# Mask rows loaded in pairs between the stores of the projected parts, and two scatters a step in the last attention group

## What is computed

```
x = ln(x + mamba(x))          # selective scan, 256 inner channels, 16 states
x = ln(x + moe_dense(x))      # 8 experts, the best 2 by softmax, plus a shared one
x = ln(x + attention(x))      # 16 heads of 8, causal
x = ln(x + moe_sparse(x))     # 64 experts, the best 4 of each token, 128 slots an expert
```

## Time and profile before

| | |
|---|---|
| runs | 1644.73, 1650.65, 1650.91 us; median 1650.65 us |
| profiled execution | 1646.96 us, its span 1645.1 us |
| granted TensorE clock, mean | 0.892 of full speed |
| busy: PE, DVE, ACT, POOL | 1332.7, 1200.2, 916.3, 943.3 us |
| scatters of line 1995 | 128, 127.3 us busy on POOL |
| affine selects of line 2011 | 128, 82.7 us busy on POOL |

### The profile page before, as it was taken

The page is one execution under the profiler, slowest core; times in us unless marked ns, Lnnn a source line. Parts: engine busy times, 40 slices in busy tenths (PEclk is TensorE's granted clock), DMA queues, the critical chain, the costliest instruction groups (busy, mean ns, idle before and its releaser), DMA issues. The chain is left out here.

```text
span 1645.1 us, 25186 instructions
## 1 busy us (share of the span) xinstructions
PE 1332.7 (81%) x7232; PEld 716.4 (44%) x7235; DVE 1200.2 (73%) x2215; ACT 916.3 (56%) x1728; POOL 943.3 (57%) x779
## 2 busy tenths in 40 slices
PE   6848888888888989999926999999999998812756
PEld 2313333333333358898913244443343343212743
DVE  6999999999999554224477988889889886260325
ACT  5746666665666554456555076675666566601423
POOL 2478899988998117360756021214563654874773
PEclk9879899999999988999957599999999999955867
DMA  2019100000000025787728211211321114301317
GB/s 70 0 59 345 56 0 0 0 0 0 0 0 0 1 61 141 205 240 199 208 55 256 60 32 37 56 31 31 83 55 35 50 35 106 60 10 47 106 51 257
DMA packets 123041, 124.87 MB, mean 76 GB/s; under 512 B 31182, under 2 KB 97979, under 8 KB 120304
## 3 DMA queue, kind: packets, MB, share of 16 engines
q1 hardware_dynamic: 101032, 99.70, 21.8%
q0 software_dynamic: 10240, 15.79, 3.3%
q10 hardware_dynamic: 11656, 8.00, 1.6%
HBM read 78.52 MB, written 50.91 MB: 79 GB/s over the span
## 5 line engine op out<-in xcount | busy, mean ns | idle before, releaser
L2106 DVE TENSOR_REDUCE t_negm<-t_ps 128x1 f32<-128x512 f32 (+4 forms) x624 | 370.0, 642 | 56.7 <-PE t_ps L2374 35.2
L2083 ACT ACTIVATE t_PT<-t_ps_s 128x1024 f32<-128x1024 f32 (+3 forms) x384 | 292.1, 811 | 203.6 <-PE t_ps_s L2393 202.6
L493 POOL TENSOR_TENSOR s_HC<-s_H,X 128x1024 f32<-128x1024 f32 x128 | 307.0, 2416 | 40.3 <-DVE s_H L614 30.1
L658 PE MATMUL ps_y<-s_HC,ident 128*128 128x512 f32 x512 | 270.5, 655 | 19.8 <-POOL s_HC L493 17.9
L2011 POOL TENSOR_SCALAR_AFFINE_SELECT t_PT<-t_PT 128x512 f32<-128x512 f32 x128 | 82.7, 646 | 276.7 <-ACT t_PT L2083 276.2
L2374 PE MATMUL t_ps<-heads 96*128 96x512 bf16 (+3 forms) x640 | 201.3, 341 | 9.4 <-DVE t_negm L2106 7.6
L2393 PE MATMUL t_ps_s<-heads 96*128 96x512 bf16 (+3 forms) x768 | 181.0, 329 | 3.7 <-ACT t_PT L2083 2.1
L2408 PE MATMUL t_ps_c<-t_PT,t_VG 128*32 128x512 f32 (+3 forms) x1536 | 164.7, 502 | 1.7 <-ACT t_CT L2039 1.1
L554 ACT ACTIVATE s_dA<-m_DT,s_A 128x512 f32 (+1 forms) x192 | 127.4, 711 | 60.3 <-DVE s_H L614 59.4
L658 PEld LDWEIGHTS ps_y<-s_HC,ident 128*128 128x128 f32 x512 | 98.4, 204 | 124.1 <-issue 69.9
L1995 POOL DMA_INDIRECT slots<-X,t_idx_s x128 | 127.3, 994 | 34.9 <-issue 34.2
(11 more groups left out here) (347 smaller groups left out, 2367.2 us busy)
## 6 DMA issues: line engine op xcount, KB each, us to landing
f_w<-in_W_dram SPq DMA_DIRECT2D x93, 256.0 KB, 5.2
heads<-token_expert_rows SPq DMA_DIRECT2D x8, 1024.0 KB, 9.6
token_expert_rows<-X SPq DMA_DIRECT2D x42, 192.0 KB, 2.6
heads<-q_parts SPq DMA_DIRECT2D x42, 192.0 KB
heads<-k_parts SPq DMA_DIRECT2D x14, 576.0 KB
expert_rows<-X SPq DMA_DIRECT2D x27, 192.0 KB, 2.5
f_XS<-expert_rows SPq DMA_DIRECT2D x19, 256.0 KB
expert_rows_out<-f_YB ACTq DMA_DIRECT2D x19, 256.0 KB, 3.6
```

What stands on the lines that cost most here:

```text
L493: nc.gpsimd.tensor_tensor(HC[:, g % RING], H[:, g % RING], row_wide(C_sb[:, g % RING, :], 2), ALU.mult).then_inc(s_hc, 2)
L658: nc.tensor.matmul(ps_y[c][:], ident[:], HC[:, g % RING, c, :], start=g == 0, stop=g == N - 1, skip_group_check=True).then_inc(s_y, 1)
L2083: nc.scalar.activation(PT[:, n % RP, 2 * p:2 * p + 2, 0:wd], src, ACT.Exp, scale=DK ** -0.5).then_inc(s_exp, 1)
L2106: nc.vector.tensor_reduce(out, ps_1[use % BANKS1][:, 0:h * width].rearrange("p (h k) -> p h k", h=h), AX.X, ALU.max, negate=True).then_inc ...
```

## The change

It changes the place of six mask loads and of twelve scatters. The loads of group 0 stay where all eight stood; those of groups 1, 2 and 3 go behind the stores of batches 0, 1 and 2. In group 15 a step may send two scatters.

```
         def _(sp):
             sp.wait_ge(keep["s_md"], 32)
-            for g in range(NG):
+
+            def mask(g):
                 for x, own_rows in enumerate((Q[g], K[g])):
                     sp.dma_start(own_rows[MASK_AT:P].rearrange("r j t -> r (j t)"), keep["mask_rows"][x]).then_inc(keep["s_mr"], 16)
+            mask(0)
             sp.wait_ge(s_z, 1)
...
                         rows = dram["k"][b, a] if x else dram["q"][b, :, a]
                         sp.dma_start(rows.rearrange("d h t -> h d t"), homes[b][:, x, a, :]).then_inc(s_d[b], 16)
+                if b + 1 < NG:
+                    mask(b + 1)
...
-                    if gi * NB + n >= (NG * (sent // (QTR * TOPK) + 1) + SCATTER[0]) * NB + SCATTER[1]:
-                        scatter(sent)
-                        sent += 1
+                    for _ in range(2 if gi + 1 == TG else 1):
+                        if gi * NB + n >= (NG * (sent // (QTR * TOPK) + 1) + SCATTER[0]) * NB + SCATTER[1]:
+                            scatter(sent)
+                            sent += 1
```

## The result

| | before | after |
|---|---|---|
| runs (us) | 1644.73, 1646.75, 1650.65, 1650.91 | 1668.44, 1670.41, 1672.47, 1673.06 |
| median | 1648.70 | 1671.44 |
| profiled execution, its span | 1646.96, 1645.1 | 1672.47, 1670.6 |
| granted TensorE clock, mean | 0.892 | 0.889 |
| GpSimd busy | 943.3 | 942.5 |

GpSimd's total says nothing of it: the same 128 scatters and 128 masks are done in the same busy time. What changed is their order, and only timelines show that.

A forecast was written before the change was run, and what follows sets the result against it. GpSimd's in-order queue was taken to bound the last group and tail, the DMA queues the projection block. 1646.96 + 14.4 + 4.0 = 1665.4, or 1669.1 from the median 1650.65; forecast between them 1667, range 1657.8 to 1671.7 us.

The forecast's parts named there:

- late last pair: Attention start: TensorE waits for all eight mask loads; the last pair lands 2.5 us after the third batch's stores.
- last mask later: Last group: eleven added scatters ahead of the last mask in GpSimd's queue make it end about 13.2 us later.
- slack: Tail: the fourth batch's first scatter could start at 1458.28 but GpSimd gets there at 1459.59; 1.3 us to win.
- clock: Start of the tail: TensorE falls to 1.2 GHz, its rows grow by at most 3.3 us; 2.5 taken.
- no room: Projection block: DMA queue full, so stores and last mask pair land later and TensorE starts the attention 5.8 us later.
- all room: Projection block: DMA queue has all the room needed, only the gain of 1.1 us in ScalarE's wait is left.
- idle share: Projection block: DMA share 0.84 leaves 0.16 of 21 us, 3.4 us; 1.8 us taken as usable.
- first batch's stores land sooner: Projection block: these stores no longer queue behind masks, so ScalarE's wait shrinks by 1.1 us at most.
- from their issue to the block's end: Projection block: four mask loads ahead of the third batch's stores make these land 5.0 us later.
- Queues with room: Projection block: first part neutral or a gain of up to 1.1 us, time 1660.3 to 1661.9; chance 0.24.
- A group that covers the scatters: Last group: masks run while scatters are worked off, the group keeps its length; 1644.6 to 1650.7 us; chance 0.08.
- Half cover: Last group and tail: scatters overlap somewhat more or the tail catches up; +5 to +10 us, 1652 to 1660; chance 0.06.

The follow-up runs named there:

- masks alone: Kernel before with only the mask loads moved in pairs between the stores, one scatter a step: 1654.85 us, ratio 1.0020.
- wait by group: Kernel before with the mask loads moved as in the change, TensorE waiting for each group's own loads by separate semaphores: 1653.68 us, ratio 1.0023.
- the clock held longer: Kernel before with two scatters a step in the last group, plus unused matmuls in its last four steps and around the context transposes: 1663.67 us, ratio 1.0085.
- the scatters placed: Kernel before with the last group's twelve scatters sent one a step, then two in steps without masks, then none: 1650.20 us, ratio 0.9991.

## Why the prediction was right

The forecast was 1667 us, slower, with ends of 1657.8 and 1671.7; the time is 1671.44, by the median 22.7 us more, where the terms summed to 18.4. In the trace the parts are 15.62 and 5.82 us, where 14.4 and 4.0 were taken. GpSimd's queue and the late last pair worked as forecast; several terms had a wrong size, and one path of the first part was missing. That the time lies inside the ends is in part luck: both parts came out above the upper ends given to them (15.2 and 5.8 us), and the upper end of the whole starts from a median of 1650.65 us, 2 us above the 1648.70 of the four runs.

**Second part, by its steps.** The last mask: 13.2 us later was forecast, 34.77 - 21.56 = 13.21 came. That is GpSimd's queue in program order, shown by taking the masks out of it. The tail then adds up from rows:

| term | forecast | measured |
|---|---|---|
| last mask later | 13.2 | 13.21 |
| GpSimd's slack ahead of the fourth batch's first scatter | -1.3 | -0.77 |
| clock | 2.5 | 2.86 |
| first scatter to the end of the block (46.58, now 46.91) | 0 | 0.33 |
| sum | 14.4 | 15.63 |

The **slack** was taken as 1459.59 - 1458.28, with 0.30 us from the weights to the scatter, the distance of two scatters in a row. A GpSimd that waits takes 0.84, so the chain could not have released it before 1457.98 + 0.84 = 1458.82: 0.77 us. The step that failed used the spacing of a busy queue for a restart after a wait. For the **clock** the sum of the rows was a little high (at most 3.3 us: 0.4, 0.4, 0.5 and 2.0 were forecast, 0.23, 0.46, 0.46 and 1.71 came), and the step "part of it lies beside ScalarE's copies" failed: nothing of these lay beside, since every row from the last product on waits for the one before it. From the last mask's end to the projection's start it is 1461.57 - 1456.50 = 5.07 us against 3.92 before, and the projection itself took 1.71 us more: 1.15 + 1.71 = 2.86. The 0.33 was not forecast: in after four scatters of the first half hold GpSimd for 1.17 to 1.22 us, where before two took 1.20 and one 1.04, all while VectorE was at work.

**First part, by its steps.** The forecast took "no room" as +5.8 and "all room" as -1.1, and took off half the idle share (half of 3.4 is 1.7, not 1.8): +4.0. The whole change showed +5.82 and the masks alone +5.12, both nearer to "no room". But the terms behind +5.8 are not those that came, and their errors cancel:

| term | forecast, no room | whole change | masks alone | wait by group |
|---|---|---|---|---|
| first batch's stores land sooner | -1.1 | none | none | none |
| third batch's stores issued later, behind ScalarE | 0 | 1.71 | 1.54 | 1.58 |
| from their issue to the block's end | 5.0 | 2.77 | 2.11 | 1.01 |
| last pair (forecast: 5.8 less the 3.9 of the block's end) | 1.9 | 1.34 | 1.47 | not waited for |
| sum | 5.8 | 5.82 | 5.12 | 2.59 |

Two steps failed. The 1.1 us that ScalarE's wait could lose were never there, since 3.7 us is the stores' plain landing time (six masks fewer ahead of them left a wait of 0.88 us). And the price of four loads, 5.0 us of queue ahead of the stores, was too high as such, while the path over ScalarE was not in the forecast: its issue of the head loads takes longer with mask loads in between and holds back chunk 4. Whether taking 1.8 us off for the idle share was wrong is not settled: the block's end moved by 2.6 to 4.5 us in three traces of the same loads. A share of 0.84, averaged over 16 engines and 4 us, did not say which.

The Trainium skill (DMA: Bandwidth & Descriptors, "Why a DMA increments its semaphore by 16 and not by 1") led to +5.8 by the rule that a transfer uses as many of 16 engines as divide its outer sizes. The total agrees with +5.82, but over other terms, so it is no test of the rule; that the head loads filled 12 of 16 engines is shown by no run here.

**The rivals.** Queues with room, 1660 to 1662: struck out by a start 5.82 us later, released by the mask rows. A group that covers the scatters: struck out by the masks that start where the second scatter ends. The Trainium skill (same page, "Anatomy of one DMA — SWDGE (gpsimd) path") would have had many descriptors go out before a cost shows; the trace disagrees with 0.97 us held for each scatter from the first pair on. Half cover: struck out by 13.21. Of the signs of being right, all came but two. TensorE's start at 909.61 lies past "901 to 906", though 3.95 us of it had passed before the first mask load; without them it is 905.66. And GpSimd's wait is 16.85 us where "about 13" was said: it has the clock term of 2.86 in it, and the restart.

**What stays open.** Why the masks alone cost 3.3 us in the times and 5.1 in the trace (the interval holds both), why the stores' landing differs by 2 us between the traces of the masks moved with one wait and with four, and why ScalarE's issue of the head loads takes longer with mask loads between the stores.

## What to carry to other kernels

An instruction that fills an idle gap on an in-order queue delays everything queued behind it: look for what other engines wait for behind it (here eight masks) before the gap, and place the filler where none follows (the steps without a mask) or take the awaited work off that engine. Before moving work forward, read the most it can win: here the fourth batch's first scatter could start at most 0.77 us earlier, against a price of 13 us. And loads that everybody waits for belong ahead of other transfers in their queue as long as they hold up nothing there (eight in front cost nothing that these traces show). Moving them between stores can also slow the issue of another engine that sends transfers, here ScalarE; a mean DMA share below 1 does not show that there is room.

## What the runs showed of the hardware

- A GpSimd scatter that waited for VectorE started 0.84, 0.85 and 0.84 us after the producing instruction ended (after, the clock held longer, the scatters placed), while scatters in a row stand 0.30 us apart.
- Some scatters held GpSimd for up to 1.22 us instead of 0.97, in the fourth batch of before and after only while VectorE was at work.
- Ahead of the eighteenth scatter of the fourth batch GpSimd stands still for 2.95 us without anything that the profile shows it to wait for, before (at 1484.46) and after (the row at 1511.20 above), and for 2.95 to 2.97 us at the same scatter in all eleven traces. No run looked into its cause; it lies on the path that sets the end.
- Issuing the same transfers took different times: a pair of mask loads took SyncE 0.80 us at the start of the block and 2.24 at 886.06, and ScalarE's three head loads 2.66 us where they took 1.32 before.
